# Channel attention in a fused layer: far maxima on VectorE, two subtractions as accumulating transfers, the bias as a weight row

## The reference, cut to what matters

```python
Q = (x @ Wq + bq).reshape(b, s, H, C) * inv_sqrt_c      # b * s = 4096 tokens; H = 16, C = 64; x has D = 256 channels
K = (x @ Wk + bk).reshape(b, s, H, C)
V = (x @ Wv + bv).reshape(b, s, H, C)
scores = jnp.einsum('bshq,bshk->bshqk', Q, K)           # 64 x 64 scores for every head of every token
mask = jnp.triu(jnp.ones((C, C), dtype=bool), 1)
w = jax.nn.softmax(jnp.where(mask, -jnp.inf, scores), axis=-1)
attn = jnp.einsum('bshqk,bshk->bshq', w, V)
x = x + attn.reshape(b, s, H * C) @ Wo + bo + ffn(xn)    # x in these products is xn, the layernorm of x
```

## Time and profile before

| | us |
|---|---|
| median of 3 runs | 3951.41 (3949.12 to 3953.07) |
| the profiled execution's own time | 3948.97 |
| its span in the trace | 3947.2 |
| start of the first attention products | 1002.46 |

### The profile page before, as it was taken

How to read it: one execution, slowest core, us unless ns; L and a number is a source line. 1 busy time by engine, 2 the same in 40 slices (tenths; PEclk the granted TensorE clock), 3 DMA queues, 4 the chain that set the end, 5 groups by cost and what they waited for, 6 DMA issues and landing times.

```text
span 3947.2 us, 72250 instructions
## 1 busy us (share of the span) xinstructions
PE 3548.3 (90%) x25960; PEld 3110.3 (79%) x26155; DVE 3260.5 (83%) x3712; ACT 1973.2 (50%) x2535; POOL 3342.6 (85%) x1498
## 2 busy tenths in 40 slices
PE   5594999966899999999999999999999999999999
PEld 4253888854688888888888888888888888888888
DVE  8332666647798899999999999899999999999988
ACT  1010333334555555555555655565555566555555
POOL 1675665622899999999999999999999999999997
PEclk8797999987999999999999999999999999999999
DMA  9323565676000000000000000000000000000000
GB/s 380 125 104 123 172 184 178 188 266 236 3 5 5 5 5 5 5 5 5 5 6 6 8 5 5 5 5 5 5 5 6 5 7 5 6 7 5 5 5 5
DMA packets 110635, 209.30 MB, mean 53 GB/s; under 512 B 16610, under 2 KB 77282, under 8 KB 110306
## 3 DMA queue, kind: packets, MB, share of 16 engines
q1 hardware_dynamic: 84192, 140.90, 11.2%
q0 software_dynamic: 21504, 59.93, 4.0%
q10 hardware_dynamic: 4608, 4.20, 0.3%
HBM read 183.34 MB, written 107.74 MB: 74 GB/s over the span
## 4 chain that ended last, share of the span: by engine, by line
POOL 37%; PE 18%; issue 15%; DVE 3%; ACT 1%; another core or an unknown queue 0%; POOLq 0%; DVEq 0%; ACTq 0%
POOL at_s L1276 34%; PE at_num L1509 7%; PE at_den L1509 6%; PE at_work L1487 3%; POOL at_m L1261 1%; POOL at_fall L1258 1%; PE at_work L1497 1%; DVE at_pv L1195 1%; DVE at_k_low L1422 1%; PE at_misc L1541 1%; PE at_misc L1535 1%; ACT at_s L1355 1%; DVE at_s L1195 1%; POOL at_m L1256 0%; DVE at_k_top L1419 0%
## 5 line engine op out<-in xcount | busy, mean ns | idle before, releaser
L1276 POOL TENSOR_TENSOR at_s<-at_s,at_m 128x2048 f32<-128x2048 f32 (+7 forms) x768 | 2511.1, 3305 | 32.6 <-DVE at_s L1195 24.5
L1355 ACT ACTIVATE at_s<-at_s 128x2048 f32<-128x2048 f32 (+7 forms) x768 | 1080.5, 1418 | 610.2 <-POOL at_s L1276 609.9
L1509 PE MATMUL at_den<-k_ident,at_s 128*128 128x128 f32 x9216 | 1135.2, 273 | 53.3 <-ACT at_s L1355 53.2
L1509 PE MATMUL at_num<-k_ident,at_pv 128*128 128x128 f32 x9216 | 1141.7, 274 | 15.8 <-issue 5.6
L1509 PEld LDWEIGHTS at_num<-k_ident,at_pv 128*128 128x128 f32 x9216 | 1048.0, 142 | 92.1 <-issue 70.3
L1509 PEld LDWEIGHTS at_den<-k_ident,at_s 128*128 128x128 f32 x9216 | 1037.0, 141 | 85.0 <-ACT at_s L1355 61.0
L1196 DVE TENSOR_TENSOR at_pv<-at_s,at_vp 128x2048 f32<-128x2048 f32 (+7 forms) x512 | 688.7, 1345 | 226.2 <-ACT at_vp L1330 179.9
L1196 DVE TENSOR_TENSOR at_s<-at_q,at_kp 128x2048 f32<-128x2048 f32 (+7 forms) x512 | 687.9, 1344 | 13.7 <-ACT at_kp L1325 10.0
L1195 DVE TENSOR_TENSOR at_pv<-at_s,at_vp 128x2048 f32<-128x2048 f32 x256 | 582.7, 2276 | 0.0
L1195 DVE TENSOR_TENSOR at_s<-at_q,at_kp 128x2048 f32<-128x2048 f32 x256 | 580.1, 2266 | 0.0
L1487 PE MATMUL at_work<-k_region,at_xT 128*128 128x512 f32 x788 | 406.0, 641 | 105.9 <-ACT at_k_far L1296 82.2
(11 more groups left out here) (232 smaller groups left out, 3396.6 us busy)
## 6 DMA issues: line engine op xcount, KB each, us to landing
moe_w<-experts SPq DMA_DIRECT2D x256, 384.0 KB
slot_x<-k_region SPq DMA_DIRECT2D x16, 2144.0 KB, 25.4
moe_x<-slot_x SPq DMA_DIRECT2D x256, 134.0 KB, 2.3
cmb_y<-picked SPq DMA_DIRECT2D x32, 768.0 KB, 7.5
at_xT<-xT SPq DMA_DIRECT2D x33, 128.0 KB, 2.0
e_x<-u SPq DMA_DIRECT2D x4, 1024.0 KB, 9.3
picked<-moe_yo,moe_row POOLq DMA_INDIRECT x256, 3.1
xT<-cmb_xT ACTq DMA_DIRECT2D x32, 128.0 KB, 5.0
```

The lines of the kernel that those rows point to most:

```text
L1276: nc.gpsimd.tensor_tensor(part(s_slot, c), part(s_slot, c), by_query(m[unit_of(c)][:], c), ALU.subtract).then_inc(sub_done, 1)
L1355: nc.scalar.activation(part(s_slot, c), part(s_slot, c), ACT.Exp, scale=C ** -0.5).then_inc(exp_done, 1)
L1509: ins = nc.tensor.matmul(dst[:, b * P:(b + 1) * P], buf[:, at:at + P], k.ident[:], start=(c in (0, NTRI) and x == 0 and b == 0), stop=Fals ...
```

## The change

**What it does.** *Far maxima*: the three POOL operations on the far queries go to DVE (`far_maxima`, both inputs in SBUF), two behind the products of chunk 3 and one behind those of chunk 4; m gets the other sign everywhere, so that it is added. *Transfers*: for chunks 11 and 16 POOL issues an accumulating DMA of -m into the `s` buffer instead of subtracting (`settle` waits for the issue of the one before); ACT waits for its landing. `show_v` of the far half moves from behind chunk 17 to behind chunk 16. *Bias*: no bias matmul. The last row of each weight matrix is taken from all its rows (DVE, `weights`), which changes nothing as the channels sum to zero and makes the last row zero; the bias is loaded into it, and channel 255 of xn is set to one. Wg and Wu, which read the same xn, lose their last row too. *Beginning*: the four large weight matrices (1 MB each) are loaded during `routed_experts`, after turns 6, 12, 18 and 24; `combine` loads the last rows, spread over the partitions (three of 256 KB, two of 384 KB), instead. The memsets clear only the leads that are read and not written, inside the main block, and the first four projections go to four banks. The code has a further switch, `FOLDED`, which is empty.

```diff
+                late = ((k.wqkv[0], "WqT"), (k.wqkv[1], "WkT"), (k.wqkv[2], "WvT"), (k.wo, "Wo"))
                 for i in range(TURNS):
                     turn_in(i)
+                    if i in (6, 12, 18, 24):
+                        dst, name = late[i // 6 - 1]
+                        sp.dma_start(dst[:], io[name].rearrange("(c p) n -> p c n", p=P)).then_inc(late_in, 16)
+                sp.wait_ge(late_in, 16 * len(late))
...
+                nc.gpsimd.memset(view(xn[:], [[D, NT]], D - 1), 1.0).then_inc(ones_set, 1)
...
-                parts = k.bias[:].rearrange("p w n -> p (w n)")
-
                 def weights(step):
                     if step == 0:
-                        dve.wait_ge(w_in, 160)
+                        dve.wait_ge(w_in, W_ALL)
                         c.mark(v.memset(k.keep_max[:], 0.0))
                         c.mark(v.memset(k.keep_min[:], 0.0))
-                        c.mark(v.memset(k.part_rows[:], 0.0))
-                        c.mark(v.tensor_copy(parts, rest[:]))
                     elif step == 1:
                         c.join()
                         c.mark(v.memset(k.keep_max[:, :, 0], -3.0e38))
                         c.mark(v.memset(k.keep_min[:, :, 0], 3.0e38))
-                        for row in (0, 64, 96):
-                            c.mark(v.memset(k.part_rows[row:row + 1, :], 1.0))
-                        c.mark(v.tensor_tensor(rest[:], rest[:], parts, ALU.subtract))
...
+                    if step < 3:
+                        w = k.wqkv[step]
+                        v.tensor_tensor(w[:], w[:], view(last[:], [[0, DC], [1, HC]], step * HC), ALU.subtract
+                                        ).then_inc(shifted, 1)
+                    elif step < 5:
+                        s = stage[step - 3][:].rearrange("p (c n) -> p c n", c=DC)
+                        c(v.tensor_tensor(s, s, view(last_up[:], [[0, DC], [1, HID]], (step - 3) * HID), ALU.subtract))
                     else:
...
-                        v.tensor_scalar(xn[:, n, :], k.x[:, n, :], mv[:, n, 0:1], rstd[:, n:n + 1],
+                        v.tensor_scalar(xn[:, n, 0:D - 1], k.x[:, n, 0:D - 1], mv[:, n, 0:1], rstd[:, n:n + 1],
...
                 for i, name in enumerate(("WqT", "WkT", "WvT")):
-                    sp.dma_start(k.wqkv[i][:], io[name].rearrange("(c p) n -> p c n", p=P)).then_inc(w_in, 16)
-                for i, name in enumerate(("bq", "bk", "bv")):
-                    sp.dma_start(rest[:, i * HC:(i + 1) * HC], io[name].partition_broadcast(P)).then_inc(w_in, 16)
-                sp.dma_start(k.wo[:], io["Wo"].rearrange("(c p) n -> p c n", p=P)).then_inc(w_in, 16)
+                    sp.dma_start(last[:, i, :], io[name][D - 1].partition_broadcast(P)).then_inc(w_in, 16)
+                for i, name in enumerate(("wgT", "wuT")):
+                    sp.dma_start(last_up[:, i, :], io[name][D - 1].partition_broadcast(P)).then_inc(w_in, 16)
...
+                sp.wait_ge(shifted, 3)
+                for i, name in enumerate(("bq", "bk", "bv")):
+                    sp.dma_start(k.wqkv[i][P - 1:P, DC - 1, :], io[name].rearrange("(o n) -> o n", o=1)).then_inc(bias_in, 16)
...
+BY_DMA = (11, 16)
...
-        with nc.Block() as block:
-            @block.gpsimd
-            def _(pool):
-                for t in (q[0], q[1], m[0], m[1]):
-                    nc.gpsimd.memset(t[:, HALF:QL], 0.0).then_inc(padded, 1)
-                for t in pv_slot:
-                    nc.gpsimd.memset(t[:], 0.0).then_inc(padded, 1)
-                pool.wait_ge(padded, 4 + PV_RING)
-            @block.vector
-            def _(dve):
-                for t in s_slot:
-                    nc.vector.memset(t[:], 0.0).then_inc(zeroed, 1)
-                dve.wait_ge(zeroed, S_RING)
+        def lead(ring, i):
+            return view(ring[i][:], [[WIDTH[i % 2], ROWS], [1, PREFIX[i % 2]]])
...
-                def maxima(t, h, step):
+                def near_maxima(t, step):
                     if step == 0:
                         pool.wait_ge(scanned, t * 4 + 4)
-                        pool.wait_ge(q_out, n + 1)
-                        nc.gpsimd.tensor_tensor(rows(m[h]), turned(k_top), rows(m[h]), ALU.mult).then_inc(max_step, 1)
+                        pool.wait_ge(q_out, t * 2 + 1)
+                        nc.gpsimd.tensor_tensor(by_row(m[0]), by_head(k_top, 0), by_row(m[0]), ALU.mult
+                                                ).then_inc(max_near, 1)
                     elif step == 1:
-                        nc.gpsimd.tensor_tensor(rows(fall), turned(k_low), rows(fall), ALU.mult).then_inc(max_step, 1)
+                        nc.gpsimd.tensor_tensor(by_row(fall), by_head(k_low, 0), by_row(fall), ALU.mult
+                                                ).then_inc(max_near, 1)
                     else:
-                        pool.wait_ge(max_step, n * 3 + 2)
-                        nc.gpsimd.tensor_tensor(m[h][:, 0:HALF], m[h][:, 0:HALF], fall[:], ALU.subtract
-                                                ).then_inc(max_step, 1)
+                        pool.wait_ge(max_near, t * 3 + 2)
+                        nc.gpsimd.tensor_tensor(m[0][:, 0:HALF], fall[:], m[0][:, 0:HALF], ALU.subtract
+                                                ).then_inc(max_near, 1)
-                MAXIMA_HERE, MAXIMA_NEXT = {2: 0, 3: 1, 4: 2}, {21: 0, 22: 1, 23: 2}
+                MAXIMA_NEXT = {21: 0, 22: 1, 23: 2}
                 GATED = 20
                 def tile(t, u):
                     for c in range(NCH):
-                        if c in (0, NTRI):
-                            pool.wait_ge(max_step, t * 6 + (3 + 3 * unit_of(c)))
+                        if c == 0:
+                            pool.wait_ge(max_near, t * 3 + 3)
+                        if c == NTRI:
+                            pool.wait_ge(max_far, t * 3 + 3)
                         pool.wait_ge(mult_done, count(t, c))
-                        nc.gpsimd.tensor_tensor(part(s_slot, c), part(s_slot, c), by_query(m[unit_of(c)][:], c),
-                                                ALU.subtract).then_inc(sub_done, 1)
-                        if c in MAXIMA_HERE:
-                            maxima(t, 1, MAXIMA_HERE[c])
+                        if c in BY_DMA:
+                            settle(pool, issued)
+                            nc.gpsimd.dma_start(part(s_slot, c), by_query(m[unit_of(c)][:], c), accum_op=ALU.add
+                                                ).then_inc(dma_done[c], 16)
+                        else:
+                            nc.gpsimd.tensor_tensor(part(s_slot, c), part(s_slot, c), by_query(m[unit_of(c)][:], c),
+                                                    ALU.add).then_inc(sub_done, 1)
                         if c in MAXIMA_NEXT:
-                            maxima(t + 1, 0, MAXIMA_NEXT[c])
+                            near_maxima(t + 1, MAXIMA_NEXT[c])
                         if c == GATED:
                             gated(t)
+                for x in (q[0], q[1], m[0], m[1]):
+                    nc.gpsimd.memset(x[:, HALF:QL], 0.0).then_inc(padded, 1)
+                for i in range(PV_RING):
+                    nc.gpsimd.memset(lead(pv_slot, i), 0.0).then_inc(padded, 1)
+                pool.wait_ge(padded, 4 + PV_RING)
                 for step in range(3):
-                    maxima(0, 0, step)
+                    near_maxima(0, step)
...
+                    if h:
+                        act.wait_ge(max_near, t * 3 + 3)
+                    else:
+                        wait(act, max_far, t * 3)
...
-                SHOW_V, SHOW_K_FAR, SHOW_K_NEXT = {1: 0, 17: 1}, 13, 21
+                SHOW_V, SHOW_K_FAR, SHOW_K_NEXT = {1: 0, 16: 1}, 13, 21
...
-                        act.wait_ge(sub_done, count(t, c))
+                        if c in BY_DMA:
+                            act.wait_ge(dma_done[c], t * 16 + 16)
+                        else:
+                            act.wait_ge(sub_done, subtracted(t, c))
...
-                keep_k(0, 0, 1)
-                keep_q(0, 0, 3)
-                keep_v(0, 4)
+                keep_k(0, 0, 1, misc)
+                keep_q(0, 0, 3, num[1])
+                keep_v(0, 4, den[1])
...
+                def far_maxima(t, step):
+                    if step == 0:
+                        dve.wait_ge(q_out, t * 2 + 2)
+                        v.tensor_tensor(by_row(m[1]), by_head(k_top, 1), by_row(m[1]), ALU.mult).then_inc(max_far, 1)
+                        v.tensor_tensor(by_row(fall), by_head(k_low, 1), by_row(fall), ALU.mult).then_inc(max_far, 1)
+                    else:
+                        dve.wait_ge(max_far, t * 3 + 2)
+                        v.tensor_tensor(m[1][:, 0:HALF], fall[:], m[1][:, 0:HALF], ALU.subtract).then_inc(max_far, 1)
...
-                OUTPUT = 14
+                OUTPUT, FAR_MAXIMA = 14, {3: 0, 4: 1}
...
                         products(t, c)
+                        if c in FAR_MAXIMA:
```

(37 more changed lines are left out.)

92 lines of the change are left out of this document (55 added, 37 removed).

## The result

The changed kernel takes 3985.48 us, median of 4 runs (3981.09 to 3986.36), beside 3951.64 of the kernel before; the ratio is 1.0084 with a 95% interval of 1.0067 to 1.0102. It is slower, as forecast, by 34 us instead of 19, and inside the range. Its profiled execution has a span of 3984.2 us, 37.0 more than before.

The account below looks back on a forecast made before the run. A ring of full PE, ACT and DVE pieces, not POOL, bounds each tile; −31 us at the beginning and +50 for +1.6 us over 31 tile distances give 3970 us from the median, range 3905 to 4015.

Parts of the forecast that it names:

- The ring: One tile's chain without slack: PE 47.16 us, ACT's piece 2.65, DVE 42.03, together 91.84; POOL has no part.
- The beginning: Before attention: shorter memsets and first projections −24 us, less weight loading in `combine` −8.8, moved loads +2; sum −31.
- The bias: Bias matmuls dropped from four projections (V, Q, V, Q) in PE's piece of the ring: 0.85 us less per tile.
- Two operations of 0.6 us ahead of `times_v`: First two far maxima on DVE wait for POOL's chunk 3 subtraction, so `times_v` of chunk 0 comes 1.4 us later.
- Q0: PE's Q projection of chunk 17, whose end is the zero for the forecast's times of POOL's operations and `times_v`.
- that distance stays: POOL's operations of chunk 2 end 18.05 us after Q0's projection, claimed unchanged because they hang on that projection.
- The third operation: Last far maximum, behind chunk 4's products in DVE's full piece: gets in before POOL and costs +0.6 us per tile.
- The clock: PE's low clock level: more idleness could bring it to more tiles, +1.7 us each; counted nothing, ±20 us for range.
- V to Q0: Piece of PE's work from chunk 11's V projection to chunk 17's Q projection; forecast −0.43 us for V and Q0 projections.
- The transfers: Accumulating DMAs for chunks 11 and 16: land in 6 to 8 us, with about 10 us of room, so cost nothing.
- the gap: Stretch between PE's and DVE's pieces, from the end of chunk 22's Q projection to `times_v` of chunk 0; before, 2.65 us.

Follow-up runs that it names:

- far_on_pool: The changed kernel with its three far maxima back on POOL behind chunks 2 to 4, both transfers kept: 3886.3 us, ratio 0.9856 to the kernel before.
- begin_and_bias: The changed kernel with far maxima and all subtractions back on POOL, leaving only the shorter beginning and the bias: 3870.0 us, ratio 0.981 to the kernel before.
- no_transfers: The changed kernel with all 24 subtractions on POOL again, far maxima still on DVE: 3973.43 us, ratio 1.0072 to the kernel before.

## Why the prediction was right, and where its sum was off

- **The ring** was right in every piece, and POOL was not the bound: two subtractions less on it gave nothing (far_on_pool against begin_and_bias), and one copy moved on ACT gave 1.8%.
- **The beginning**, −31: measured −32.4. **The bias**, −0.85 a tile: −0.88 where V's projection is at the low clock, −0.57 where it is at the high one.
- **Two operations of 0.6 us ahead of `times_v`, held until chunk 3's subtraction ends (+1.4 against Q0)** was the mis-sized term. By the prediction's own measure `times_v` should have moved from 19.6 to 21.0 us after Q0's projection; it starts 22.5 us after it, +2.9. Two steps failed. The duration was taken from a row with plain access (0.68); these read k_top and k_low turned, and take 1.06. And DVE was to wait once, behind chunk 3, since "that distance stays", 18.05 us from Q0's projection to the end of chunk 2. It did not stay: 19.2 us in the mean. Before, ACT had been idle when Q0's projection came (0.90 us in the mean) and took it 0.35 us after its end; now PE is earlier, ACT is still busy with exponentials (0.00 idle) and takes it after 1.43. So DVE's first operation queued behind chunk 2, POOL's chunk 3 queued behind DVE's first, and DVE's second behind chunk 3: 0.5 and 1.5 us of waiting instead of one wait.
- **The same, where V is at the low clock,** came nearly as forecast: PE reaches Q0 later, ACT takes it 0.20 us after its end, chunk 2 ends at 18.0 and chunk 3 at 19.8 (forecast 19.8), and `times_v` starts at 21.5. Such a tile takes 93.9 us in no_transfers (forecast 93.4); one at the high clock 93.3, where the forecast had 91.7. The size that failed is that of the tile at the high clock.
- **The third operation**, +0.6: +0.51, and it got in first.
- **The clock**, counted at nothing with more low clock feared: V's projection was at the low clock in 21 of 30 tiles before (granted 0.56 in the earlier trace rows) and in 1 after, and took 1.98 us in the mean instead of 2.77. With what follows it, the piece from V to Q0 had been 1.69 us longer at the low clock (28.26 against 26.57), so it shrank by 1.11 in the mean. Not all of that was a gain, since `times_v` comes about 1.0 us later against Q0 in a tile at the high clock: the whole tile differs by 0.65 (no_transfers), about 0.4 us a tile in the mean. Why the clock stayed high is not shown.
- **The transfers**, at nothing: 0.26 us a tile here, 0.43 with far maxima on POOL. Their latency was sized well (7.8 us); the room of 10 us, read from one tile, was not there in every tile.

Together: −32.4, and 2.16 us in each of 30 tile distances (65), and the first and last tiles' share (about 5) make the span's +37.0. Per tile the forecast had +1.57; its errors are +1.5 for the gap and −0.9 for V to Q0 (clock and transfers), which partly cancelled. The direction came from the mechanism that was forecast; that the total came within 15 us is in part luck with the clock.

## What to carry to other kernels

Find the ring of full pieces between engines and add it up to the tile's time; an engine outside it can be busy for 96% and still be worth nothing when relieved. Before moving work onto a ring's engine, ask whose instructions it takes turns with during just that stretch: one operand in PSUM instead of SBUF was worth 1.9 us a tile here. A distance read in one tile can be another in the tiles at the other clock; read both kinds. Look first for copies that stand in the ring only by their place in the program; moving one gave 1.8% here, where the whole change lost 0.8%.
